# One dense group's experts moved to the front of the last block, with the second sorted set's routing among them

## The reference

```
h2     = layernorm(h) ; p = softmax(h2 @ router_weight.T)        # 8 experts
keep   = the two largest of p per token (ties to the lower expert)
out[t] = x[t] + h[t] + sum over kept e of p[t,e] * (gelu(h2[t] @ w1[e]) @ w2[e])   # 128 -> 256 -> 128
```

## Time and profile before

| | us |
|---|---|
| median of 3 runs (lowest, highest) | 853.35 (845.95, 854.05) |
| the profiled execution, its own time | 853.38 |
| its span on the core | 851.6 |
| TensorE busy | 665.0 (78%) |
| VectorE busy | 604.7 (71%) |
| ScalarE busy | 389.2 (46%) |
| GpSimd busy | 309.2 (36%) |
| causal attention's last products to the first product of the last block | some 668 to 701 |
| last block | 695.3 to 851.6 |

### The profile page before, as it was taken

How to read it: one execution, slowest core, us unless ns; L and a number is a source line. 1 busy time by engine, 2 the same in 40 slices (tenths; PEclk the granted TensorE clock), 3 DMA queues, 4 the chain that set the end, 5 groups by cost and what they waited for, 6 DMA issues and landing times. The chain is left out here.

```text
span 851.6 us, 25368 instructions
## 1 busy us (share of the span) xinstructions
PE 665.0 (78%) x9768; PEld 497.6 (58%) x9768; DVE 604.7 (71%) x1672; ACT 389.2 (46%) x843; POOL 309.2 (36%) x448
## 2 busy tenths in 40 slices
PE   3468988889697898889999567777876508898995
PEld 1345555555465776777778335555555407787884
DVE  7568877977877988998998466787867635344264
ACT  3022333223243665667665445666653316556441
POOL 3332122332425033212200364555513746427372
PEclk9968999999897999999999769999997758999898
DMA  4000000041025211222110510000000123325232
GB/s 105 8 15 22 24 22 22 20 94 26 13 86 126 78 39 53 79 80 74 43 56 14 155 53 4 4 4 3 4 4 12 43 74 94 107 79 152 73 103 69
DMA packets 61285, 45.46 MB, mean 53 GB/s; under 512 B 11820, under 2 KB 56568, under 8 KB 61176
## 3 DMA queue, kind: packets, MB, share of 16 engines
q1 hardware_dynamic: 55064, 36.66, 15.5%
q0 software_dynamic: 3072, 6.30, 2.4%
q10 hardware_dynamic: 3040, 0.98, 0.5%
HBM read 20.85 MB, written 18.87 MB: 47 GB/s over the span
## 5 line engine op out<-in xcount | busy, mean ns | idle before, releaser
L984 ACT ACTIVATE P<-bank 128x512 f32<-128x512 f32 x128 | 76.6, 598 | 75.3 <-PE bank L1130 74.1
L1056 DVE TENSOR_SCALAR bank<-bank 128x512 f32<-128x512 f32 x128 | 88.9, 695 | 16.9 <-PE bank L1121 15.9
L1064 DVE TENSOR_REDUCE mx<-bank 128x4 f32<-128x512 f32 x128 | 87.1, 681 | 0.7 <-PE bank L1104 0.6
L500 ACT ACTIVATE w2r<-bank 128x512 f32<-128x512 f32 x40 | 23.9, 597 | 113.9 <-PE bank L814 79.0
L2328 PE MATMUL bank<-w2r,hme 128*128 (+1 forms) x512 | 70.6, 282 | 0.2
L2328 PEld LDWEIGHTS bank<-w2r,hme 128*128 128x128 f32 x512 | 65.5, 194 | 6.7 <-issue 1.7
L973 POOL TENSOR_TENSOR inv_sum<-inv_sum,dn 128x16 f32<-128x16 f32 x32 | 7.1, 221 | 164.6 <-DVE dn L1085 146.9
L1130 PE MATMUL bank<-mT,negsel 128*128 128x128 f16 x512 | 51.1, 223 | 13.5 <-DVE bank L1056 12.1
L1834 POOL DMA_INDIRECT sorted_x<-xsrc,pos x48 | 47.3, 986 | 31.3 <-DVE pos L2045 17.4
L2172 POOL DMA_INDIRECT ZT<-sorted_y,pos x48 | 46.0, 958 | 26.9 <-issue 14.2
L416 POOL TENSOR_TENSOR rn<-n,half 128x8 f32<-128x8 f32 x8 | 13.8, 1720 | 106.2 <-DVE n L639 106.2
(11 more groups left out here) (456 smaller groups left out, 1970.7 us busy)
## 6 DMA issues: line engine op xcount, KB each, us to landing
sorted_x<-zero SPq DMA_DIRECT2D x2, 2048.0 KB
Yq<-sorted_x SPq DMA_DIRECT2D x16, 256.0 KB, 3.4
sorted_y<-Yq SPq DMA_DIRECT2D x16, 256.0 KB, 2.5
cross_q<-qh SPq DMA_DIRECT2D x24, 128.0 KB
Q<-cross_q SPq DMA_DIRECT2D x8, 384.0 KB, 3.9
X<-in_x SPq DMA_DIRECT2D x8, 256.0 KB, 2.8
Xq<-X SPq DMA_DIRECT2D x32, 64.0 KB
cross_k<-kh SPq DMA_DIRECT2D x16, 128.0 KB
```

The lines of the kernel that those rows point to most:

```text
L984: act.activation(P[j][:], TB[u % 3][:], ACT.Exp, scale=SCALE).then_inc(s["p_ready"], 1)
L1056: dve.tensor_scalar(TB[(U * b + j) % 3][:], TB[(U * b + j) % 3][:], -CLIP, CLIP, ALU.max, ALU.min).then_inc(s["t_clip"], 1)
L1064: dve.tensor_reduce(mx[:, 4 * j:4 * j + 4], SB[j % 2][:].rearrange("p (h k) -> p h k", h=4), AX.X, ALU.max).then_inc(s["s_max"], 1)
```

## The change

Groups 3 and 7 become the dense ones, and the sets are 0, 1, 2 and 4, 5, 6. The last block's list begins with the 8 dense items of group 3, then come all 16 sorted units without a break, then the 8 items of group 7. attention2 ends two steps sooner (q up to 33): it now does second halves of groups 0 to 4 only (and the normalisation of group 5), the gate of group 3 instead of a set's logits, routing parts 0 to 7 of set 0 and its first 16 sends. The rest goes into the last block: sends 16 to 23 at GpSimd's start, routing parts 8 and 9 of set 0 at VectorE's start, second halves of groups 5 and 6 from block 0, the whole routing of set 1 at the blocks in `ROUTE` (parts 0 to 6 in blocks 5 to 14, the count on TensorE at 12), both halves of group 7 from block 8. Set 1's sends come after group 7's root and sum on GpSimd. SyncE's program is one loop over 16 units, with the store of unit u ahead of the load of u + 3; group 3 is stored behind unit 7, group 7 ahead of the last sorted group. The diff, cut to its core (index changes that follow from the new numbering are left out):

```diff
--- before.py
+++ after.py
@@ attention2 @@
-        PLACES = {0: (0,), 1: (2, 3), 3: (6,), 8: (7,), 9: (8,), 10: (9,)}
-        SENDS = {27: range(2), 28: range(2, 5), 29: range(5, 8), 30: range(8, 10), 31: range(10, 14), 32: range(14, 19),
-                 33: range(19, 24)}
+        PLACES = {0: (0,), 1: (2, 3), 3: (6,), 8: (7,)}
+        SENDS = {27: range(2), 28: range(2, 5), 29: range(5, 8), 30: range(8, 10), 31: range(10, 14), 32: range(14, SENT)}
...
-            return g if k == at and 0 <= g < NSP else None
+            return g if k == at and 0 <= g < LAST - 1 else None
...
-                for q in range(FIRST, QUADS + 4):
+                for q in range(FIRST, QUADS + 2):
...
+                    if q == QUADS:
+                        expert_normalise(act, e, H, LAST - 1)
...
-                    if q == QUADS + 3:
-                        place_exp(act, e, 1)
+                    if q == 28:
+                        expert_exp(act, e, 0)
...
+                    if q == QUADS:
+                        expert_gate(dve, e, LGS, DENSE[0], 3)
+                        expert_gate(dve, e, LGS, DENSE[0], 4)
...
+                    if q == QUADS - 1:
+                        expert_gate(dve, e, LGS, DENSE[0], 2)
+                    if q == QUADS + 1:
+                        expert_stats(dve, e, H, PX, LAST, 1)
...
-                    if second_half(q, 3) is not None:
+                    if second_half(q, 3) in DENSE:
+                        expert_gate(dve, e, LGS, second_half(q, 3), 0)
+                    elif second_half(q, 3) is not None:
                         gather_logits(dve, e, LGS, second_half(q, 3))
...
-                    if q == QUADS + 3:
-                        place(dve, e, None, 1, 0)
@@ constants @@
-SETS, DENSE = ((0, 1, 2), (3, 4, 5)), (6, 7)
+SETS, DENSE = ((0, 1, 2), (4, 5, 6)), (3, 7)
...
-STARTS = {6: -4, 7: 22}
-BCUT = 3
-FINISH = (40, 44, 48, 56, 61)
+SENT = 16
+STARTS = {5: -5, 6: -3, 7: 8}
+ROUTE = {5: (0,), 7: (1,), 8: (2,), 9: (3,), 10: (4,), 13: (5,), 14: (6,), 20: (7,), 22: (8,), 24: (9,)}
+GATES = {15: 0, 26: 2, 27: 3, 28: 4}
+FINISH = (41, 46, 51, 59, 66)
@@ experts1 @@
-    ITEMS[BCUT:BCUT] = [("s", u, None) for u in range(NU, 2 * NU)]
-    ITEMS[0:0] = [("s", u, None) for u in range(NU)]
+    ITEMS[NE:NE] = [("s", u, None) for u in range(2 * NU)]
...
-                for n in range(2):
-                    for v in range(3):
-                        load(NU * n + v)
-                    for v in range(NU):
-                        if v + 3 < NU:
-                            load(NU * n + v + 3)
-                        keep_y(NU * n + v)
-                sp.wait_ge(s["combined"], DONE[DENSE[0]])
-                store(DENSE[0])
-                for g in SETS[0]:
-                    sp.wait_ge(q["done"], g + 1)
-                    store(g)
-                sp.wait_ge(s["combined"], DONE[DENSE[1]])
-                store(DENSE[1])
-                for g in SETS[1]:
-                    sp.wait_ge(q["done"], g + 1)
+                for u in range(3):
+                    load(u)
+                for u in range(2 * NU):
+                    keep_y(u)
+                    if u + 3 < 2 * NU:
+                        load(u + 3)
+                    if u == NU - 1:
+                        sp.wait_ge(s["combined"], DONE[DENSE[0]])
+                        store(DENSE[0])
+                for at, g in enumerate(SORTED):
+                    if at == NSP - 1:
+                        sp.wait_ge(s["combined"], DONE[DENSE[1]])
+                        store(DENSE[1])
+                    sp.wait_ge(q["done"], at + 1)
                     store(g)
...
-                expert_send(pool, e, 1, range(2 * NT))
+                expert_send(pool, e, 0, range(SENT, 2 * NT))
                 expert_root(pool, e, DENSE[1])
                 expert_sum(pool, e, X3, H, DENSE[1])
+                expert_send(pool, e, 1, range(2 * NT))
                 back(0)
                 back(1)
...
-                expert_normalise(act, e, H, DENSE[0])
-                slots_high(0)
                 for k in range(BLOCKS):
...
-                    for g in jobs(k, 8):
-                        expert_exp(act, e, DENSE.index(g))
+                    if k == 6:
+                        place_exp(act, e, 1)
+                    if k == 16:
+                        expert_exp(act, e, 1)
...
-                for p in range(1, 7):
-                    place(dve, e, PRE, 1, p)
-                slots_low(0)
+                for p in (8, 9):
+                    place(dve, e, None, 0, p)
...
-                    if k in (5, 7, 9):
-                        place(dve, e, PRE, 1, 7 + (k - 5) // 2)
+                    for p in ROUTE.get(k, ()):
+                        place(dve, e, PRE, 1, p)
...
-                    for p in (4, 3, 2, 0):
-                        for g in jobs(k, 7 + p):
-                            expert_gate(dve, e, LG, g, p)
+                    for g in jobs(k, 7):
+                        if g not in DENSE:
+                            gather_logits(dve, e, LG, g)
+                    if k in GATES:
+                        expert_gate(dve, e, LG, DENSE[1], GATES[k])
...
-                place_count(pe, e, PRE, 1)
-                choose(0)
-                slots_turn(0)
                 for k in range(BLOCKS):
...
+                    if k == 12:
+                        place_count(pe, e, PRE, 1)
```

More of the change, by code:

```diff
@@ L1293, in quads @@
             return t[:, 4 * n:4 * n + 4, :]
-        FIRST, ROUTED, COUNTED, LATE = -12, 24, 26, 4
+        FIRST, ROUTED, COUNTED, LATE, LAST = -12, 24, 26, 4, 6
         EARLY = {1: (1,), 2: (4,), 3: (5,)}
-        PLACES = {0: (0,), 1: (2, 3), 3: (6,), 8: (7,), 9: (8,), 10: (9,)}
-        SENDS = {27: range(2), 28: range(2, 5), 29: range(5, 8), 30: range(8, 10), 31: range(10, 14), 32: range(14, 19),
-                 33: range(19, 24)}
+        PLACES = {0: (0,), 1: (2, 3), 3: (6,), 8: (7,)}
+        SENDS = {27: range(2), 28: range(2, 5), 29: range(5, 8), 30: range(8, 10), 31: range(10, 14), 32: range(14, SENT)}
         def first_half(q, at):
             g, k = q // 4 - 2, q % 4
-            return g if k == at and 0 <= g <= NSP else None
+            if q > QUADS:
+                return LAST if q == QUADS + 1 and at == 2 else None
+            return g if k == at and 0 <= g <= LAST else None
         def second_half(q, at):
             g, k = q // 4 - 3, q % 4
-            return g if k == at and 0 <= g < NSP else None
+            return g if k == at and 0 <= g < LAST - 1 else None
         with nc.Block() as block:
@@ L1535, in step @@
                         expert_stats(dve, e, H, PX, first_half(q, 0), 0)
-                    if first_half(q, 2) is not None:
+                    if first_half(q, 2) is not None and q < QUADS:
                         expert_stats(dve, e, H, PX, first_half(q, 2), 1)
+                    if q == QUADS:
+                        expert_gate(dve, e, LGS, DENSE[0], 3)
+                        expert_gate(dve, e, LGS, DENSE[0], 4)
                     if k == 1 and n + 2 >= 1 and chunk(n + 2):
@@ L1645, in widen @@
                     after(pe, s["xT_lo"], min(n + 3, G))
-                    after(pe, e["s"]["ph_ready"], min(n, NSP + 1))
+                    after(pe, e["s"]["ph_ready"], min(n, LAST + 1))
                     rv = RB[:].rearrange("p (a j s) -> p j a s", a=2, s=T)
@@ L1719 @@
 EXPERT_RING = 8
-SETS, DENSE = ((0, 1, 2), (3, 4, 5)), (6, 7)
-NSP = sum(len(t) for t in SETS)
+SETS, DENSE = ((0, 1, 2), (4, 5, 6)), (3, 7)
+SORTED = SETS[0] + SETS[1]
+NSP = len(SORTED)
 NT = GB * len(SETS[0])
@@ L1734, in turned @@
 def turned(t, g, lo=0, n=N):
-    at = N * (g % 2 if g < NSP else g - NSP + 2) + lo
+    at = N * (2 + DENSE.index(g) if g in DENSE else g % 2) + lo
     return t[:, at:at + n]
@@ L1742, in set_of, with row_of @@
     return next(k for k, groups in enumerate(SETS) if g in groups)
+def row_of(g):
+    return GB * SORTED.index(g)
 def expert_state(nc, room, keep):
@@ L1756, in expert_state @@
         "r16": keep["expert"]["r16"], "rb": keep["expert"]["rb"], "b1": keep["expert"]["b1"], "ones": keep["ones"],
-        "steps": [0],
+        "steps": [0], "c8": sb("c8e", [128, 3, GB, NE, NE]),
         "xsrc": sb("xsrc", [S, GB * NSP, C]), "zero": sb("zero", [128, C]), "tri": sb("tri", [128, 128]),
@@ L1841, in normalised @@
         return lambda i: e["xn"][:, i, :]
-    return lambda i: e["xsrc"][:, GB * g + i, :]
+    return lambda i: e["xsrc"][:, row_of(g) + i, :]
 def expert_normalise(act, e, H, g, tiles=range(GB)):
@@ L1951, in gather_logits @@
     s, n = e["s"], set_of(g)
-    at = GB * g - NT * n
+    at = row_of(g) - NT * n
     dve.wait_ge(s["lg_psum"], g + 1)
@@ L2097, in experts1 @@
         YS = [stage[:, N * (4 + i):N * (4 + i) + N] for i in range(4)]
-        xh = [keep["causal"]["K_all"][:, 4 * N * i:4 * N * i + 4 * N] for i in range(2)]
         xh = [sb(f"xhs{i}", [C, 4 * N], F16) for i in range(2)]
```

(14 more changed lines are left out.)

23 lines of the change are left out of this document (13 added, 10 removed).

## The result

The changed kernel takes 905.93 us (median of four runs, 902.55 to 909.91) where the kernel before takes 851.48 beside it: a ratio of 1.0651, with an interval of 1.0578 to 1.0723. The forecast was 918.5 with a range of 893 to 945, so the direction and the range hold and the forecast is 12.6 us too high.

What follows compares the result with a forecast made beforehand. Bounds seen: an idle gap near 690 us, the sorted copy-store-load-turn loop, and a tail of gathers and stores. First copy 728.3, plus 140.7, 6.3, 41.4 and 1.8 around the span, gave 918.5 us; range 893 to 945.

Steps and rivals of the forecast that it cites:

- SyncE's order: Sorted loop: storing u before loading u+3 makes the way from copy through turn to next copy paid every unit, 10.82 us.
- block starts: Start of the last block, after attention ends two steps sooner: at 684.7 us, 10.6 us earlier than before.
- from there to the first copy: Last block's start to first sorted copy: 33.9 us of dense items and routing plus two sorted units, 9.7 us.
- 13 units: Sorted units whose turns 3 to 15 wait for a load: 10.82 us each, 140.7 in all (129 to 164).
- last two copies: End of the sorted part: the last two copies come at 6.3 us together, as in the kernel before.
- last copy to end of span: Tail after the sorted part, set by GpSimd's gathers: 41.4 us where it was 48.9, saving 7.5.
- Dense items first: Front of last block: group 3's eight dense items fill the gap, taking 24.6 to 33.9 us; 33.9 taken.
- quiet price: Sorted loop: time from a copy to the waiting TensorE turn while GpSimd is quiet, 4.32 us.
- rival 2: Sorted units: full clock throughout and no contention, 13 x 9.9 us, giving 906.5 us; chance 0.22.
- Rival 1: Sorted units: loads stay hidden with three ahead, 4.87 us per unit, giving 844.6 us, or 835; chance 0.06.
- Rival 3: Sorted units: gathers and low clock in every unit, 13 x 12.6 us, giving 942 us; chance 0.12.
- Rival 4: Last block doesn't start earlier, from VectorE's added gates or another late barrier: 10 us more, 929 us; chance 0.10.

Runs made afterwards that it cites:

- load_first: The changed kernel with SyncE loading unit u+3 ahead of storing unit u, so four loads are ahead; 842.73 us, ratio 0.9896 to the kernel before.
- old_items_store_first: The kernel before with only SyncE's order changed, the store of unit v ahead of the load of v+3; 898.87 us, ratio 1.0549.
- load_at_copy: The changed kernel with SyncE waiting for the copy of unit u, then loading u+3, then storing u; 903.63 us, ratio 1.0623 to the kernel before.
- load_at_copy_clock: The changed kernel with the load ahead of the store at the copy, plus 14 extra TensorE products before each wait; 890.11 us, ratio 1.0483.
- loads_early: The changed kernel with loads issued as soon as their buffer is free, not held behind stores; 837.66 us, ratio 0.9845 to the kernel before.

## Why the prediction was right

**The mechanism.** Everything that the prediction put on SyncE's order came: 13 waits (13 forecast), 58.5 us in all (60), a store and a load as a pair every 10.3 us (10 to 12), first copy at 721.56 (718 to 735). load_first and old_items_store_first show the order of store and load to be the cause, load_at_copy and load_at_copy_clock that the store's place ahead of the load in the queue is the smaller part of it (with the clock held, 10.0 us per unit fall to 9.2), and loads_early that the number of buffers is not the cause.

**The terms.** Forecast 918.5, profiled execution 904.95; the 13.5 us between them are these:

| term | forecast | measured | difference |
|---|---|---|---|
| block starts | 684.7 | 682.4 | -2.3 |
| from there to the first copy | 43.6 | 39.2 | -4.4 |
| 13 units | 140.7 | 134.0 | -6.7 |
| last two copies | 6.3 | 6.8 | +0.5 |
| last copy to end of span | 41.4 | 40.9 | -0.5 |

*Start.* The step holds: the first late send was at 669.12 in the old trace and at 666.71 in this one, 2.4 us sooner. From that send to the start of the block it is 15.7 us, where 15.6 were forecast. In the profiles of the nine kernels with the new items the send lies between 662.85 and 667.78, in the three with the old items between 668.32 and 669.12: some of the 2.4 us may be the change, some is scatter, and what does it was not traced.

*Dense items first.* I took the upper end of 24.6 to 33.9, with all of set 1's routing exposed. The measured 39.2 less two sorted units of 4.87 is 29.4, the middle: the bounds held, and the choice was 4.4 us too high. That part of the routing lies beside the items after all is the likely reason; it was not tested by itself.

*The unit.* This is the largest miss, 10.82 against 10.31. From copy to turn I had 4.75. Beside sends it is 4.27 and 4.32, no more than quiet, where I had 4.51. Three turns beside set 0's gathers take 4.80, 5.29 and 4.98, where I had 6.05 from two rows before. The one ahead of them takes 4.54: the gathers begin only 0.6 us before it, but group 3's four stores, which I had costed at nothing, are issued right behind its load. The quiet price, 4.32, held: the other seven take 4.10 to 4.48. That price came from a fourth wait in the kernel before, 1.28 us at 752.95, which my 5.4 us of waits there left out (it is 6.7). From turn to copy I took 6.07 as the middle of 5.60 and 6.54; the mean is 5.85, from 5.34 to 6.33.

*The clock.* It falls to 0.50 once in each of the 13 units, as the earlier trace rows had it for the wait of 3.04 us: in six units up to 2.7 us ahead of the turn, in seven up to 1.1 us behind its start. So a price between the two rows was right in kind, and 0.22 us per unit too high. The rule of the Trainium skill (TensorE: Matmul & The Clock Gate, section on HAM oscillation) is that work which waits for a DMA per tile restarts at the low clock each time. The changed kernel agrees in part: the mean granted clock from 721 to 851 us is 0.79, but seven of the 13 turns start ahead of the fall. load_at_copy agrees in full, with a clock of 0.66 and all 13 turns behind the fall.

*Tail.* The last gather is issued 32.6 us after the last copy (32.9 forecast), the finish follows 2.6 later; GpSimd is the bound there, as said.

**The rivals.** The time lies nearer to rival 2 (906.5) than to the forecast, but not for its reason: it wanted full clock in every unit, and the clock was at 0.79. The unit of 10.31 us lies halfway between rival 2's 9.9 and the forecast's 10.82; a start and a dense part that were cheaper than forecast bring the sum to rival 2, and that closeness is luck. Rival 1's condition failed, since copy to turn and turn to copy together take 10.3; its time was right for loads that are hidden by other means: in loads_early a unit takes 5.1 us and the kernel 837.66, between its 835 and 844.6. Rival 3 charged the gathers in every unit; only three turns lay beside them, at 5.0 us on average and not at 6.05. Rival 4's late start didn't come.

**The range.** Two of its ends don't come out of the terms. With the ends given for the block's start and for the dense items, the first copy would lie between 716.3 and 738.6, not 718 and 735; and rival 2 with a first copy at 718 gives 896, not 893. The measured values lie inside either way.

## What to carry to other kernels

Where one queue stores a result and loads an input, count how many tiles of work lie between a load's issue and its use: moving the load behind the store of the same round took that from one tile to none, and a few lines cost 62 us. Issue loads by when their buffer comes free, not by when a result leaves: with the same four buffers that took 13 waits down to one. And price a repeated wait with what the engine's clock does behind it, by a row where it waited for about as long.

## What was unexpected of the hardware

A shorter wait that leaves TensorE idle can be worth nothing. Issuing the load 0.7 us sooner in each of 13 units changed neither the unit (10.28 against 10.31 us) nor the time (903.63 against 905.93), since turn to copy grew by 0.67 at a granted clock of 0.66 instead of 0.79. With the clock held by products that nobody reads, the same early load was worth its price: 9.2 us per unit and 890.11. Ten such products per wait in the changed kernel held it little (0.84, 906.54), 17 did (0.99, 901.77). What in the activity of the engine decides when in a unit the clock falls was not tried further and stays open.
